# One small product folded in two, GpSimd's first work re-timed, and six products of ones at the start of a fused transformer kernel

## The chip, the cores and the metric

The kernel runs on one core of one Trainium2 chip. The time is device microseconds of one launch; less is better. Three runs of the kernel before gave 958.53, 959.26 and 959.52 us, median 959.26.

## What is computed

A whole decoder block stack in float32: four layers of attention with a feed-forward part, a cross attention, and a feed-forward part whose weights are put together from the 32 chosen of 64 primitives. Cut to what matters here:

```python
x = layernorm(x + attn_layers(x))        # 4 layers: local + linear attention, then gelu MLP
x = layernorm(x + cross_attention(x, ctx))
x = layernorm(x + composed_ffn(x))

def compose_weight(logits, A, B):        # "the choice", 64 logits, 32 taken
    vals, idx = top_k(logits, 32)
    w = softmax(vals)
    return einsum('k,kir,kro->io', w, A[idx], B[idx])
```

The choice depends on 64 logits alone, so the kernel makes it early, between the first attention's products, and uses its weights some 650 us later.

## The kernel before

Every engine runs a program written out by hand, and semaphores tie them together; nothing is scheduled by a tool. 2048 tokens are worked in four items of 512. Float32 products are made of three passes over a high part and a low part: ScalarE or GpSimd writes the high part, VectorE or GpSimd the low part (the "splits": `split_wo`, `split_lo`, lines L412 and L418).

`first_step` and `second_step` hold the first two items of layer 0, and beside them all the work that is done once. The order of instructions on an engine is the order in the code, so an engine that waits holds up everything behind it. The parts that matter here:

- **VectorE, `first_step`.** `top_choose` finds the rank of each logit and, last, writes `chosen` in two instructions (L782); their semaphore step is `top_step` 6. Then comes the reciprocal of the softmax sums of item 0 (L717). `top_weigh` follows: two instructions on the choice's sums and places in PSUM (L788, L789), `lw` (L792: product of two 64x2 tiles in SBUF), and `weighted` in two instructions (L795: SBUF to SBUF, by a scalar of each row), whose step is `top_w` 1. Behind them stand the low part of the linear attention (L635, one source in PSUM) and four copies of transposed probabilities out of PSUM (L713).
- **TensorE, `first_step`.** `top_k` (L1645, L1647) sums and gathers for the choice. Then the transposes of the first half's probabilities (`pe_pt`, L1559), then a wait for `index_ready` and for `top_w` 1, then `pe_pnorm` (L1566), the second half's transposes, a projection, `pe_pv` (L1576), two more projections, and `top_columns` (L1654), which spreads `weighted` over the partitions.
- **GpSimd.** After constants and the second item's `rstd` it waits for the choice, splits Wo (L412 twice, L418 twice), writes the low part of W1 (L418 four times) and adds the bias bo to item 0 (`pool_bias`, L470). The bias is needed by `dve_res1` (L733).
- **VectorE, `second_step`.** `dve_features` of item 1 begins with the query's maximum (L664) and the subtraction of it (L666, two sources in SBUF), whose step is `qsub_done` 2; this is "the query pass". Behind them are the score maxima out of PSUM (L707, L708), then L671 (SBUF to SBUF), L673, L676, L678 and L680. L680 releases TensorE's `pe_qnt` (L1526). L691 releases `pe_lin` (L1550), L631 the transposes of the second norm (L1453).
- **TensorE's beginning.** `pe_busy` (L1621) multiplies the bf16 identity by itself into PSUM; nobody reads the result. Seven such products wait for `const_step` 8, five more for the first `rstd`, and three follow the first transposes (L1638).

Of the kernel before, what the change touches and what calls it, by code (L numbers as in the profile page):

```python
# [19 lines left out]
P = 128  # L20
# [22 lines left out]
def build(nc, x_in, Wq, Wk, Wv, Wo, bo, ln1_g, ln1_b, W1, b1, W2, b2, ln2_g, ln2_b,  # L43
          ctx_in, Wkv, Wout, bout, fc1_A, fc1_B, fc2_A, fc2_B, fc1_logits, fc2_logits, out):
    with ExitStack() as ctx:
        def sb(name, shape, dt=F32):
            return ctx.enter_context(nc.sbuf_tensor(name, shape, dt))

        def sem(name):
            return ctx.enter_context(nc.semaphore(name))  # L50
# [21 lines left out]
        ones = sb("ones", [P, 1])  # L72
# [28 lines left out]
        weighted = top[:, 384:448].rearrange("p (f n) -> p f n", f=2)  # L101
        ones64, earlier = top[:, 640:768], top[:, 768:832]
# [35 lines left out]
        def f_ht(p, i, m):  # L138
# [3 lines left out]
            if i == 0:  # L142
# [5 lines left out]
        F = ctx.enter_context(nc.psum_tensor("F", [P, 2, 512], F32))  # L148
# [8 lines left out]
        const_step, const_ready, zero_ready = sem("const_step"), sem("const_ready"), sem("zero_ready")  # L157
# [14 lines left out]
        qmax_done, qsub_done, qexp_done, kexp_done = sem("qmax_done"), sem("qsub_done"), sem("qexp_done"), sem("kexp_done")  # L172
# [16 lines left out]
        logits_loaded, top_const, top_step, top_exp, top_w, top_idx, top_wcol, index_ready = (  # L189
            sem(n) for n in ("logits_loaded", "top_const", "top_step", "top_exp", "top_w", "top_idx",  # L190
                             "top_wcol", "index_ready"))
# [19 lines left out]
        def slot(p):  # L211
            return slice(TILES * p, TILES * p + TILES)

        def w1_part(k):


            c, s = k // 2, k % 2

            def dst(i):
                return w1[:, i, c, :].rearrange("q (m p) -> q p m", p=P)[:, 64 * s:64 * s + 64, :]  # L220
            return dst, A[:, k, :].rearrange("q (p m) -> q p m", m=FC)
# [15 lines left out]
        def cross_bank(u):  # L237
            return F[:, u - 2, :] if 2 <= u < 4 else A[:, u + 4 if u < 2 else u - 4, :]
# [49 lines left out]
        def _(sp):  # L288
# [49 lines left out]
            def indices(first):  # L338

                _, values = nc.values_load_multi_w_load_instructions(  # L340
                    index[0:1, bass.ds(first, 8)], engines=[mybir.EngineType.SP], min_val=0, max_val=PRIMS - 1,
                    skip_runtime_bounds_check_because="VectorE holds every index between 0 and PRIMS - 1 as it writes them")
                return values
# [70 lines left out]
        def split_lo(pool, pieces, hi_sem, ready, l):  # L414

            for k, (hi, low, src) in enumerate(pieces):
                pool.wait_ge(hi_sem, len(pieces) * l + k + 1)
                last = pool.tensor_tensor(low, src, hi.bitcast(F32), ALU.subtract)  # L418
            last.then_inc(ready, 1)
# [12 lines left out]
        def split_wo(pool, l, n=None):  # L432
            pool.wait_ge(raw_wo_loaded, 16 * (l + 1))
            if n is not None:
                pool.wait_ge(wo_psum, 2 * n + 2)
            split(pool, [(wo[:, 0, c, :], wo[:, 1, c, :], raw_a[:, c, 768:1024]) for c in range(DC)], wo_hi, wo_ready, l)
# [7 lines left out]
        def w1_pieces():  # L444
            hi, low = (w1[:, i].rearrange("p c n -> p (c n)") for i in range(2))
            return [(hi[:, a:a + TOK], low[:, a:a + TOK], raw_f[:, a:a + TOK]) for a in range(0, 2048, TOK)]
# [18 lines left out]
        def pool_bias(pool, i, n, p):  # L465

            vec = (vec_a, vec_f)[i]
            pool.wait_ge(ln_ready[i], TILES * (n + 1))
            pool.wait_ge(bias_loaded[i], 16 * (n // ITEMS + 1))
            pool.tensor_tensor(x[:, slot(p), :], x[:, slot(p), :], vec[:, 2:3, :].broadcast_to([P, TILES, D]),  # L470
                               ALU.add).then_inc(biased[i], 1)
# [7 lines left out]
        def _(pool):  # L479
# [36 lines left out]
            pool_rstd(pool, 0, 1)  # L516
            pool.wait_ge(zero_ready, 1)
            pool.wait_ge(top_const, 8)
            pool.wait_ge(top_w, 1)
            split_wo(pool, 0)  # L520
            split_lo(pool, w1_pieces(), w1_hi, w1_ready, 0)
            pool_bias(pool, 0, 0, 0)

            def step(l, p, attn=True, nxt=True, mlp=True, out=True):
# [54 lines left out]
            for k in range(4):  # L579
                dst, _ = w1_part(k)  # L580
                pool.wait_ge(comp_hi, k + 1)
                last = pool.tensor_tensor(dst(1), w1_raw[:, k, :].rearrange("q (p m) -> q p m", m=FC), dst(0).bitcast(F32),
                                          ALU.subtract)
# [1034 lines left out]
        def pe_busy(pe, bank, count):  # L1618

            for _ in range(count):  # L1620
                pe.matmul(bank.rearrange("p (k n) -> p k n", k=4), ident_bf[:, :],  # L1621
                          ident_bf[:, :].rearrange("p (o n) -> p o n", o=1).broadcast_to([P, 4, P]), start=True, stop=True)

        @block.tensor
        def _(pe):
            pe.wait_ge(const_step, 8)
            pe_busy(pe, F[:, 1, :], 7)
            pe.wait_ge(const_ready, 1)
# [20 lines left out]
            def top_columns():  # L1649
                pe.wait_ge(top_w, 1)  # L1650
                pe.wait_ge(tok_out, 5)
                for j in range(2):
                    for f in range(2):
                        last = pe.matmul(F[:, 0, 32 * j + 16 * f:32 * j + 16 * f + 16], ones64[:, :],  # L1654
                                         weighted[:, f, :].rearrange("i (k j) -> i j k", j=2)[:, j, :], start=True, stop=True)
                last.then_inc(top_wcol_psum, 1)

            def wvt_turn(k):
# [15 lines left out]
            def first_step():  # L1674
# [39 lines left out]
                pe_tok(pe, 1, 2)  # L1714
                pe_tok(pe, 1, 3)
                top_columns()
                pe_s(pe, 1, 0)
                pe.wait_ge(tok_out, 8)
# [200 lines left out]
            for u in range(2 * ITEMS):  # L1919
# [6 lines left out]
                for i in range(2):  # L1926
                    last = pe.matmul(cross_bank(u)[:, D:2 * D], pick[:, u:u + 1].broadcast_to([P, P]), mean_row[i],
                                     start=i == 0, stop=i == 1)
# [68 lines left out]
```

## Time and profile before

| | |
|---|---|
| median of 3 runs | 959.26 us (958.53 to 959.52) |
| the profiled execution's own time | 958.49 us |
| its span, first to last instruction | 956.3 us |
| TensorE busy | 944.4 us, 99% |
| VectorE, ScalarE, GpSimd busy | 673.6, 611.8, 480.2 us |
| chain that ended last | 94% TensorE, 3% VectorE, 1% ScalarE, 1% issue |

How to read it: the 2.2 us between the span and the own time lie around the instructions. The chain that ended last is followed back from the last instruction, so a microsecond taken off a part of the chain counts in full until a second chain of nearly the same length shows up. All that the change touches lies in the first 62 us; after that the program is the same.

### The profile page before, as it was taken

The numbers are of one execution on the slowest core, as the hardware profiler recorded it, in microseconds if no ns is written. First come the engines' busy times: TensorE is split into PE (matmuls) and PEld (weight loads), VectorE is DVE, ScalarE is ACT, GpSimd is POOL, SyncE is SP. The second block draws the span as 40 slices with busy tenths as digits, with TensorE's granted clock in tenths as the row PEclk, the third lists the DMA queues.
The fourth block names the chain that finished last, engine by engine and source line by source line (L and its number), as shares of the span: only waits on it lengthen the run. The fifth ranks groups of instructions, "written<-read, shape, count | busy, mean of one in ns | idle before, by whom it ended". The sixth has DMA issues, their size and how long they took to land.

```text
span 956.3 us, 21341 instructions
## 1 busy us (share of the span) xinstructions
PE 944.4 (99%) x8394; PEld 815.6 (85%) x8394; DVE 673.6 (70%) x1529; ACT 611.8 (64%) x1389; POOL 480.2 (50%) x381
## 2 busy tenths in 40 slices
PE   7999999999999999999999999999999999999998
PEld 4688888888888889888888888888997889998997
DVE  7796868677777868696777678776662776666445
ACT  4777777686776867777768677686856345444220
POOL 3437375456826472775466367816247224006453
PEclk9999999999999999999999999999999999999999
DMA  6231000001110000021000003000028696820001
GB/s 211 72 108 45 2 17 2 8 11 58 33 45 19 2 1 19 1 89 45 10 9 1 18 2 84 4 2 7 2 57 204 137 205 143 181 46 1 23 23 45
DMA packets 71582, 47.56 MB, mean 50 GB/s; under 512 B 44511, under 2 KB 68159, under 8 KB 71487
## 3 DMA queue, kind: packets, MB, share of 16 engines
q1 hardware_dynamic: 71487, 46.27, 18.9%
q8 instruction: 63, 1.03, 0.4%
q14 instruction: 32, 0.26, 0.1%
HBM read 44.16 MB, written 2.10 MB: 48 GB/s over the span
## 4 chain that ended last, share of the span: by engine, by line
PE 94%; DVE 3%; ACT 1%; issue 1%; DMA 0%; POOL 0%; SPq 0%; POOLq 0%; DVEq 0%; ACTq 0%
PE F L1460 21%; PE F L1614 19%; PE A L1460 16%; PE A L1802 5%; PE A L1795 5%; PE A L1559 4%; PE A L1955 4%; PE A L1517 3%; PE F L1474 2%; PE A L1576 2%; PE A L1474 2%; PE F L1453 2%; PE A L1550 1%; PE A L1453 1%; PE A L1533 1%; PE A L1526 1%
## 5 line engine op out<-in xcount | busy, mean ns | idle before, releaser
L1460 PE MATMUL F<-xt,w 128*128 128x512 f32 x864 | 217.8, 400 | 0.2 <-ACT scratch L1211 0.2
L475 POOL TENSOR_TENSOR ht<-scratch,ht 128x512 fp32r<-128x512 f32 x128 | 176.2, 1397 | 29.4 <-ACT ht L1214 27.9
L1460 PEld LDWEIGHTS F<-xt,w 128*128 128x128 f32 x864 | 157.6, 188 | 38.2 <-issue 3.0
L1614 PE MATMUL F<-w,ht 128*128 128x256 f32 x1536 | 188.8, 282 | 0.0
L1614 PEld LDWEIGHTS F<-w,ht 128*128 128x128 f32 x1536 | 182.8, 188 | 5.3 <-issue 4.6
L463 POOL TENSOR_TENSOR rstd<-var,minus_half 128x4 f32<-128x4 f32 x32 | 37.6, 1173 | 176.4 <-DVE var L611 175.8
L1211 ACT ACTIVATE scratch<-F,b_now 128x512 f32<-128x512 f32 x128 | 87.6, 684 | 36.6 <-POOL ht L475 19.0
L1460 PE MATMUL A<-wa,xt 128*128 128x512 f32 x372 | 89.8, 397 | 0.0
L470 POOL TENSOR_TENSOR x<-x,vec_f 128x1024 f32<-128x1024 f32 x16 | 38.0, 2376 | 93.7 <-DVE scratch L631 93.7
L1214 ACT ACTIVATE ht<-scratch 128x512 fp32r<-128x512 f32 x128 | 80.9, 632 | 4.1
L1460 PEld LDWEIGHTS A<-wa,xt 128*128 128x128 f32 x372 | 69.0, 188 | 15.9 <-issue 0.2
L631 DVE SCALAR_TENSOR_TENSOR scratch<-scratch,rstd,vec_a 128x256 f32<-128x256 f32 x64 | 70.3, 1158 | 0.2
L1182 ACT ACTIVATE prob<-A,smax 128x128 f32<-128x128 f32 (+1 forms) x128 | 51.9, 432 | 21.5 <-DVE smax L708 21.5
L1149 ACT ACTIVATE scratch<-A 128x256 f32<-128x256 f32 x62 | 23.7, 382 | 63.8 <-PE A L1460 63.5
L635 DVE TENSOR_TENSOR xt<-A,xt 128x512 fp32r<-128x512 f32 x52 | 33.5, 685 | 39.2 <-ACT xt L1134 34.4
L733 DVE TENSOR_TENSOR x<-A,x 128x512 f32<-128x512 f32 x30 | 20.7, 692 | 54.4 <-PE A L1460 54.4
L1444 ACT ACTIVATE scratch<-F 128x512 f32<-128x512 f32 x32 | 19.2, 600 | 54.1 <-PE F L1460 48.4
L1182 ACT ACTIVATE scratch<-A,smax 128x128 f32<-128x128 f32 (+1 forms) x128 | 51.9, 434 | 0.4
L740 DVE TENSOR_TENSOR x<-F,x 128x256 f32<-128x256 f32 x64 | 26.4, 420 | 32.3 <-PE F L1614 32.3
L563 POOL TENSOR_TENSOR trstd<-tvar,minus_half 128x4 f32<-128x4 f32 (+1 forms) x15 | 13.3, 887 | 68.2 <-DVE tvar L835 68.2
L603 DVE BATCH_NORM_STATS2 stats<-x 128x6 f32<-128x256 f32 x128 | 44.8, 413 | 2.2 <-DMA x<-in_x_dram 1.6
L1460 PEld LDWEIGHTS A<-wo,at 128*128 128x128 f32 x360 | 43.3, 188 | 1.3
(264 smaller groups left out, 2041.9 us busy)
## 6 DMA issues: line engine op xcount, KB each, us to landing
raw_f<-in_L_attn_W_dram SPq DMA_DIRECT2D x8, 1024.0 KB, 5.5
scratch<-in_L_ffn_fc_B_dram SPq DMA_DIRECT2D x32, 256.0 KB, 4.2
scratch<-in_L_ffn_fc_A_dram SPq DMA_DIRECT2D x32, 256.0 KB, 4.0
raw_f<-in_L_ffn_fc_A_dram SPq DMA_DIRECT2D x32, 64.0 KB, 3.4
scratch<-in_x_dram SPq DMA_DIRECT2D x1, 2048.0 KB, 10.1
raw_f<-in_L_ffn_fc_B_dram SPq DMA_DIRECT2D x32, 64.0 KB, 3.2
x<-in_x_dram SPq DMA_DIRECT2D x3, 512.0 KB, 3.7
out_dram<-x SPq DMA_DIRECT2D x3, 512.0 KB, 2.9
```

Source lines behind the costliest of these rows:

```text
L475: pool.tensor_tensor(ht[:, 1, m, :], hf[:, m % 2, :], ht[:, 0, m, :].bitcast(F32), ALU.subtract).then_inc(h_lo, 1)
L603: last = dve.bn_stats(stats[i][:, t, :], x[:, TILES * p + t, :])
L631: dve.scalar_tensor_tensor(out=xh[i][:, t, :], in0=xh[i][:, t, :], scalar=rstd[i][:, t:t + 1], in1=vec[:, 1, :], op0=ALU.mult, op1=ALU.add ...
L1182: last = act.activation(prob[b][:, h, a:z], A[:, 2 + h, a:z], ACT.Exp, bias=smax[:, b, w, h:h + 1], scale=-1.0, accum_out=psums[:, 2 * b + ...
L1211: act.activation(hf[:, m % 2, :], F[:, m % 2, :], ACT.Gelu, bias=b1_now[:, m:m + 1]).then_inc(gelu_done, 1)
L1214: act.activation(ht[:, 0, m, :], hf[:, m % 2, :], ACT.Copy).then_inc(h_hi, 1)
L1460: last = pe.matmul(out, lhs(a, c), rhs(b, c), start=clear and k == 0, stop=k == len(total) - 1, skip_group_check=not clear)
L1474: last = pe.matmul(out, lhs(a, c), rhs(b, c), start=k == 0, stop=k == len(total) - 1)
L1559: last = pe.transpose(A[:, PT_BANKS[b][r], P * h:P * h + P], prob[b][:, h, P * r:P * r + P], ident[:, :])
L1614: last = pe.matmul(F[:, t % 2, 0:D], ht[:, a, c, P * t:P * t + P], w2[:, b, c, :], start=k == 0, stop=k == len(passes) - 1)
L1795: last = pe.matmul(A[:, 2 * c + s, :], small[r][a][:, P * c:P * c + P], big[r][b][:, 512 * s:512 * s + 512], start=first and k == 0, stop= ...
L1802: last = pe.matmul(A[:, m // 2, D * (m % 2):D * (m % 2) + D], big[r][a][:, P * m:P * m + P], small[r][b], start=first and k == 0 and m % 2 ...
```

## The change

Four edits. GpSimd's first split waits for `top_step` 6 (the ranks' `chosen`) where it waited for `top_w` 1 (the finished weights). GpSimd's first bias sum waits for `qsub_done` 2 as well. TensorE begins with six products of a column of ones, spread with stride 0 to 128x128, as soon as the ones are written (`const_step` 1). And `top_columns` makes one product of 32 columns for each half `j` where it made two of 16 columns (two `matmul` calls instead of four; a float32 product leaves two records, so four records instead of eight).

```diff
             pool_rstd(pool, 0, 1)
             pool.wait_ge(zero_ready, 1)
             pool.wait_ge(top_const, 8)
-            pool.wait_ge(top_w, 1)
+            pool.wait_ge(top_step, 6)
             split_wo(pool, 0)
             split_lo(pool, w1_pieces(), w1_hi, w1_ready, 0)
+            pool.wait_ge(qsub_done, 2)
             pool_bias(pool, 0, 0, 0)
...
         @block.tensor
         def _(pe):
+            pe.wait_ge(const_step, 1)
+            for _ in range(6):
+                pe.matmul(F[:, 1, 0:P], ones[:, :].broadcast_to([P, P]), ones[:, :].broadcast_to([P, P]), start=True, stop=True)
             pe.wait_ge(const_step, 8)
             pe_busy(pe, F[:, 1, :], 7)
...
                 for j in range(2):
-                    for f in range(2):
-                        last = pe.matmul(F[:, 0, 32 * j + 16 * f:32 * j + 16 * f + 16], ones64[:, :],
-                                         weighted[:, f, :].rearrange("i (k j) -> i j k", j=2)[:, j, :], start=True, stop=True)
+                    last = pe.matmul(F[:, 0, 32 * j:32 * j + 32].rearrange("p (f k) -> p f k", f=2), ones64[:, :],
+                                     weighted[:, :, :].rearrange("i f (k j) -> i j f k", j=2)[:, j], start=True, stop=True)
                 last.then_inc(top_wcol_psum, 1)
```

On GpSimd, from the constants of the mask to the second norm's bias, with the semaphores that each instruction waits for:

```order
 L514 AFFINE_SELECT mask_seed<-mask_seed 128x128 x2
 L463 TENSOR_TENSOR rstd<-var,minus_half 128x4 [waits ln1_var]
-L412 TENSOR_TENSOR wo<-raw_a,ones 128x256 [waits top_w,raw_wo_loaded,top_const,zero_ready]
+L412 TENSOR_TENSOR wo<-raw_a,ones 128x256 [waits top_step,raw_wo_loaded,top_const,zero_ready]
 L412 TENSOR_TENSOR wo<-raw_a,ones 128x256
 L418 TENSOR_TENSOR wo<-raw_a,wo 128x256 [waits wo_hi] x2
 L418 TENSOR_TENSOR w<-raw_f,w 128x512 [waits w1_hi] x4
-L470 TENSOR_TENSOR x<-x,vec_a 128x1024 [waits bo_loaded,ln1_ready]
+L470 TENSOR_TENSOR x<-x,vec_a 128x1024 [waits bo_loaded,ln1_ready,qsub_done]
```

No instruction of GpSimd moved against another; two of them wait for something else.

On TensorE around `top_columns`, in the kernel before (the last projection ahead of it is L1460, the scores of item 1 behind it L1510 and L1517):

```order
L1460 MATMUL A<-wa,xt 128x512 [waits aloc_done]
L1460 MATMUL A<-wa,xt 128x512 x5
L1654 MATMUL F<-scratch 128x16 [waits tok_out,top_w]
L1654 MATMUL F<-scratch 128x16 x3
L1510 MATMUL A<-mask_bf,ident_bf 64x2x128 x8
L1517 MATMUL A<-kT,qT 128x128 x4
```

and in the changed kernel:

```order
L1461 MATMUL A<-wa,xt 128x512 [waits aloc_done]
L1461 MATMUL A<-wa,xt 128x512 x5
L1657 MATMUL F<-scratch 128x32 [waits tok_out,top_w]
L1657 MATMUL F<-scratch 128x32
L1511 MATMUL A<-mask_bf,ident_bf 64x2x128 x8
L1518 MATMUL A<-kT,qT 128x128 x4
```

Two of the four products went, and the two that stay have twice the columns.

## Rows read from the trace of the kernel before

**Rows 1.** The page: the span.
```profile
span 956.3 us, 21341 instructions
```

**Rows 2.** Chain that ended last, 33 to 62 us: start us, us, what.
```profile
33.09 0.04 issue
33.13 0.87 PE A L1550 x48
...
37.47 0.44 PE A L1566 x4
...
45.05 0.99 PE F L1654 x8
```

**Rows 3.** Timeline of TensorE: start us, us, instructions.
```profile
37.30 0.60 PE L1566 MATMUL A<-ident,scratch 128*128 128x128 f32 x4
...
52.67 0.60 PE L1526 MATMUL A<-ident,scratch 128*128 128x128 f32 x4
...
61.69 1.05 PE L1453 MATMUL F<-ident,scratch 128*128 128x128 f32 x8
```

**Rows 4.** Timeline of VectorE, the choice.
```profile
34.48 0.37 DVE L782 TENSOR_SCALAR scratch<-places,rank 64x32 f32<-64x32 f32 x2
...
36.25 0.14 DVE L792 TENSOR_TENSOR lw<-lexp,lsum 64x2 f32<-64x2 f32 x1
36.43 0.38 DVE L795 TENSOR_SCALAR scratch<-scratch,lw 64x32 f32<-64x32 f32 x2
```

**Rows 5.** Timeline of GpSimd, its first splits and bias sum.
```profile
37.04 1.18 POOL L412 TENSOR_TENSOR wo<-raw_a,ones 128x256 fp32r<-128x256 f32 x2 [18.65 <-DVE scratch L795]
38.18 1.43 POOL L418 TENSOR_TENSOR wo<-raw_a,wo 128x256 fp32r<-128x256 f32 x2
39.55 5.04 POOL L418 TENSOR_TENSOR w<-raw_f,w 128x512 fp32r<-128x512 f32 x4
44.55 2.81 POOL L470 TENSOR_TENSOR x<-x,vec_a 128x1024 f32<-128x1024 f32 x1
```

**Rows 6.** Timeline of VectorE, item 1's query pass and what follows.
```profile
46.50 1.40 DVE L666 TENSOR_TENSOR scratch<-scratch,qmax 128x512 f32<-128x512 f32 x1
...
49.69 0.41 DVE L671 TENSOR_SCALAR scratch<-scratch 128x512 f32<-128x512 f32 x1
...
51.74 0.69 DVE L680 TENSOR_TENSOR scratch<-scratch,qsum 128x512 f32<-128x512 f32 x1
...
59.91 1.67 DVE L631 SCALAR_TENSOR_TENSOR scratch<-scratch,rstd,vec_f 128x256 f32<-128x256 f32 x4
```

**Rows 7.** VectorE's L611 by itself: ns min/median/max, first and last start.
```profile
L611 DVE TENSOR_SCALAR var<-mv x32: 169/170/622, 5.5 to 706.3; 128x4 f32<-128x4 f32 x32
```

**Rows 8.** Timelines of VectorE and GpSimd at three meetings later in the run.
```profile
88.50 0.62 DVE L611 TENSOR_SCALAR var<-mv 128x4 f32<-128x4 f32 x1
87.78 1.31 POOL L418 TENSOR_TENSOR w<-raw_f,w 128x512 fp32r<-128x512 f32 x1
...
228.95 1.54 DVE L671 TENSOR_SCALAR scratch<-scratch 128x512 f32<-128x512 f32 x1
228.93 1.28 POOL L418 TENSOR_TENSOR w<-raw_f,w 128x512 fp32r<-128x512 f32 x1
...
71.36 0.48 DVE L631 SCALAR_TENSOR_TENSOR scratch<-scratch,rstd,vec_a 128x256 f32<-128x256 f32 x1
71.35 1.64 POOL L475 TENSOR_TENSOR ht<-scratch,ht 128x512 fp32r<-128x512 f32 x1
```

**Rows 9.** TensorE's beginning: its timeline, then a stretch's sums (granted clock after POOL's).
```profile
3.44 3.17 PE L1621 MATMUL F<-ident_bf 128*128 128x512 bf16 x7 [3.44 <-POOL ident_bf L490]
7.14 1.84 PE L1621 MATMUL F<-ident_bf 128*128 128x512 bf16 x5 [0.54 <-POOL rstd L463]
9.44 1.63 PE L1638 MATMUL A<-ident,scratch 128*128 128x128 f32 x8 [0.46 <-DVE scratch L631]
...
3.40:6.70 3.30, 3.17 (x7) 0.88 (x7) 2.01 (x10) 0.00 (x0) 2.78 (x9) 1.00 0.76 215
```

## The prediction, made before the changed kernel ran

> **What bounds the kernel now.** I began with the page: a span of 956.3 us [rows 1], and TensorE at 99% busy. A kernel like that gains only what leaves TensorE's own queue, and loses whatever makes TensorE wait. So the second view was the chain that ended last, over the stretch that the change touches [rows 2]. The reader is to see that from 33.13 us, when the wait for VectorE's context ended ("issue" 0.04), to 61.85 us it is TensorE alone, product after product. Third came the timelines of TensorE, VectorE and GpSimd side by side at the places of the edits [rows 3 to 6], to see how much room each releaser has. Fourth, meetings of VectorE and GpSimd elsewhere in the run [rows 7, 8], since the edits put GpSimd's work beside other instructions of VectorE.
>
> **A. `top_columns`.** It leaves eight records in 0.99 us of the chain [rows 2], 0.124 each. Four go: 0.50 us. The four that stay have 32 columns instead of 16; L1566's transposes have 128 columns and take 0.44/4 = 0.11 each [rows 2], so the wider columns cost between nothing and nothing visible. TensorE is on the chain here, so 0.5 us comes off, for as long as nobody else is late. ScalarE's copy of the weights behind it comes earlier too, and waits for nothing else.
>
> **B. GpSimd's splits come earlier.** L782 ends at 34.48 + 0.37 = 34.85 [rows 4]. Today L795 ends at 36.81 and the first split starts at 37.04 [rows 4, 5], 0.23 later. With the same 0.23 it will start at 35.08, 1.96 earlier. Nobody waits for the splits: the product with Wo starts at about 48 us, so the earliness itself earns nothing. What counts is who is met. By the durations of [rows 5], L412 runs 35.08 to 36.26, the two L418 on Wo 36.22 to 36.95 and 36.91 to 37.65, the first on W1 37.59 to 38.88, and all is done by 42.6.
>
> VectorE has L792 at 36.25 and L795 at 36.43 [rows 4], between `top_k` and the wait at which TensorE wants `top_w`. What does it cost to meet GpSimd? [Rows 8] show it. L611, a small SBUF to SBUF operation of 0.17 us by itself [rows 7], takes 0.62 at 88.50 and ends at 89.12, just after GpSimd's L418 (87.78 + 1.31 = 89.09). L671, 0.41 by itself [rows 6], takes 1.54 at 228.95 and ends at 230.49, 0.28 after GpSimd's 228.93 + 1.28 = 230.21. So VectorE's instruction is held until GpSimd's ends, and then needs its own duration less about 0.13. Who starts first decides: L671 started 0.02 behind GpSimd's and lost; L631 at 71.36, 0.01 behind GpSimd's 71.35, took its plain 0.48, and GpSimd's took 1.64.
>
> The Trainium skill speaks against this edit: its GPSIMD Engine Reference, § 1 Specifications, says that GpSimd's SBUF interfaces are shared with VectorE, with contention for VectorE instructions that have two SBUF inputs or run in a two-port mode. The trace agrees for L611 and L671, which have a single tensor in SBUF. If only two-input instructions were held, L792 alone would pay, and the sum below would shrink to the second rival's 0.5 us.
>
> Step by step then. L792 wants to start at 36.25, 0.03 behind L418's 36.22: nearer to the lost meeting (0.02) than to the won one (0.01), so it is held to 36.95 and ends at 36.95 + 0.14 - 0.13 = 36.96. The first L795 needs `lw`, so it starts at 36.99, 0.08 behind the second L418 (36.91): held to 37.65, done at 37.65 + 0.23 - 0.13 = 37.75. (0.23 is the pair's 0.38 less the 0.15 by which its starts lie apart.) The second L795 starts about 0.08 before that, at 37.67, 0.08 behind the first W1 split (37.59): held to 38.88, done at 38.98. TensorE's L1566, which starts at 37.30 today [rows 3], starts 0.05 after that (the 0.04 of "issue", rounded up [rows 2]): 39.03. **That is a new wait of 1.73 us on the chain.** Bounds: nothing, if VectorE wins each meeting (TensorE is only 0.45 behind `top_w` now: 36.81 + 0.05 against 37.30); 2.4 us if a GpSimd instruction is itself stretched by 0.3 as at 71.35 on the way, twice. Behind L795 on VectorE stand L635 and the L713 copies, which have PSUM sources. The first L713 would end near 40.1; the second half's last transposes, which wait for it and start 1.3 us after L1566, come at 40.3. So nothing is added there; everything behind moves by 1.73 as a block.
>
> **C. The bias sum behind the query pass.** Now it runs from 44.55 to 47.36 [rows 5], and L666 takes 1.40 [rows 6], 0.7 of it held (46.50 until 47.36). L666 will take 0.69. But the bias sum then starts 0.2 after it, at 47.19 + 0.2 = 47.4 (on the old clock), and runs about 2.4 us (2.81 less the 0.4 for which VectorE's L635 had just cut in) to 49.8. The score maxima read PSUM and pass. L671 comes 0.7 earlier, at 49.0, meets it, and ends at 49.8 + 0.41 - 0.13 = 50.05 instead of 50.10. So of 0.7 us VectorE keeps 0.05 to 0.1: the stall goes from L666 to L671. ScalarE does get its exponentials 0.7 earlier, which nobody waits for.
>
> That limits A. L680 ends at 52.43 now and releases L1526 at 52.67 [rows 3, 6], a slack of 0.24 with 0.05 taken by the release. Half a microsecond earlier, TensorE would want L680 by 52.12, and gets it at 52.35 + 0.05 = 52.40: A keeps 0.27 of its 0.5. VectorE works without a break from there, and L631 ends at 61.58 now against L1453 at 61.69: 0.06 of slack. Ended 0.08 earlier it lets TensorE be 0.14 earlier. **A and C together: -0.15 us** (between 0 and -0.5, if the bias sum does not meet L671).
>
> **D. Six products of ones.** TensorE stands idle until 3.44 [rows 9]; they fill 0.97 to about 3.6 (12 records of a float32 product at twice the 0.11 of A, since the engine is slow here). The seven fillers take 0.43 each, (3.17 - 0.61)/6, and of the five after them the last are quicker; the granted clock of that stretch reads 1.00, so what was really granted must be told from durations: the slower level (1.2 GHz) until after 8 us, the faster one (2.4 GHz) at 9.44. The transposes there wait for VectorE. So in this execution D earns nothing; it costs nothing while the fillers still end before 7.1, and they do with 0.4 to spare.
>
> The Trainium skill's TensorE: Matmul & The Clock Gate, Part 1, says that how many products are slow at a kernel's start varies from run to run. Here it would mean that some runs before paid in their first real products and the changed kernel does not; one trace can't show that.
>
> **Sum.** +1.73 - 0.15 + 0 = +1.6 us. Against the profiled execution's own 958.49 that is 960.1. The median of the three runs is 0.77 above it, and I take that difference to stay: 959.26 + 1.6 = **960.8 us**. A change within 0.2%, 1.9 us, is about what measurement of this kernel can't tell from none; so the forecast is "no difference", on its slow side.
>
> **Rivals.**
> - *The main case*, TensorE waits 1.7 us for `top_w`: +1.6, spread 0.5. For it: both rows of lost meetings, and lags of 0.03, 0.08, 0.08. Against it: the first lag is two hundredths from a won one, and a start that moves by 0.03 turns it. Chance 45%.
> - *One or two meetings won*: L792 wins its meeting, one L795 is held by the first Wo split, the other by the second. `top_w` at 37.65 + 0.1 = 37.75, TensorE at 37.80 instead of 37.30: +0.5 - 0.15, about 959.6. Chance 22%.
> - *No wait at all*, because such small tiles slip in: only A and C are left, -0.15 to -0.5, 958.9. Chance 18%. If the runs before also lose time to a slow start that D removes, 958.4, since their own spread is 1.0 us.
> - *The other side, slower by over 0.2%*: a clock that falls. With the ones ahead, the fillers may end by 5.5 us, and TensorE then stands idle to 7.14 and again to 9.44, or it idles 1.7 us at 37.3; if it is then back at the slower level, the first projections (24 or so of 0.235 us that would take 0.43) cost 2.5 us or more. It decides from about ten slow products on. For it: the idle stretches grow. Against it: no gap of 0.5 to 0.75 us had this effect in the first 12 us. Chance 8%, 962 to 963.
> - *Something that I did not see*: 7%, half on each side.
>
> **How the numbers follow.** Of the main case 30% lies over +1.9 us (a start or two more of 0.15 to 0.3), which with the clock gives slower 0.14 + 0.08 + 0.03 = 0.25. Faster by over 0.2% needs no wait, all of A and a slow start in the median: 0.08. The rest, 0.67, is no difference. The range leaves out the falling clock and the luckiest end: 958.6 to 962.0.
>
> **What would show it.** Right: GpSimd's first L412 at 35.1; L792 or L795 at several times 0.14 and 0.23; L1566 with an idle stretch released by VectorE's `weighted`; L666 at 0.69 and L671 near 1.0; the bias sum near 2.4 us; four records of `top_columns` in 0.5 us; L1526 waiting for L680. Wrong: L795 at its plain duration with GpSimd's split running, no idle in front of L1566, or fillers and first transposes at other durations than now.

## The result

The changed kernel takes 960.74 us, median of 14 runs (959.95 to 962.46), against 958.93 of 14 runs of the kernel before (957.81 to 959.77). The ratio is 1.0023, 95% interval 1.0016 to 1.0030: slower, by about the 0.2% that was called the bound of what can be told. Fourteen runs of each tell it from none all the same. The forecast of 960.8 us lies 0.06 from the median. The profiled execution took 962.04 us, near the top of its runs, with a span of 959.9; why it lies above the median comes out below. Two executions of the experiments' lots, at 1155.24 and 1869.04 us, stand far outside and are left out of every ratio and count below.

The page of the changed kernel begins:

```profile
span 959.9 us, 21357 instructions
PE 947.1 (99%) x8402; PEld 818.1 (85%) x8402; DVE 675.1 (70%) x1529; ACT 611.5 (64%) x1389; POOL 479.2 (50%) x381
```

TensorE is busy 2.7 us more than before with eight records more, and the span grew by 3.6 us [rows 1]. Where it went is read from the chain that ended last, 33 to 62 us, that answers to [rows 2] (start us, us, what):

```profile
34.80 0.87 PE A L1551 x48
...
37.67 1.46 PE A L1560 x12
39.13 1.54 issue
40.67 0.63 PE A L1567 x4
...
48.45 0.56 PE F L1657 x4
...
55.72 0.12 issue
55.84 0.63 PE A L1527 x4
```

L1567 is L1566 of before. In front of it stands 1.54 us of "issue", where before nothing stood. `top_columns` takes 0.56 instead of 0.99, and a small wait of 0.12 in front of L1527 (L1526 of before) is new. "issue" says that the trace names no releaser: the wait is for `index_ready` and `top_w`, which a sequencer's instruction takes. Who was late is seen on VectorE. Its timeline in the changed kernel, and below it GpSimd's:

```profile
37.92 0.71 DVE L793 TENSOR_TENSOR lw<-lexp,lsum 64x2 f32<-64x2 f32 x1
38.67 1.90 DVE L796 TENSOR_SCALAR scratch<-scratch,lw 64x32 f32<-64x32 f32 x2
40.49 0.54 DVE L636 TENSOR_TENSOR at<-A,at 128x384 fp32r<-128x384 f32 x1
...
36.75 1.18 POOL L412 TENSOR_TENSOR wo<-raw_a,ones 128x256 fp32r<-128x256 f32 x2 [17.45 <-DVE scratch L783]
37.89 1.42 POOL L418 TENSOR_TENSOR wo<-raw_a,wo 128x256 fp32r<-128x256 f32 x2
39.27 5.00 POOL L418 TENSOR_TENSOR w<-raw_f,w 128x512 fp32r<-128x512 f32 x4
50.67 2.40 POOL L470 TENSOR_TENSOR x<-x,vec_a 128x1024 f32<-128x1024 f32 x1 [6.41 <-DVE scratch L667]
```

L793 (before: L792) takes 0.71 instead of 0.14, and the two L796 (before: L795) 1.90 together instead of 0.38 [rows 4]. The second L796 and the W1 split that it meets, each by itself:

```profile
39.27 1.30 DVE L796 TENSOR_SCALAR scratch<-scratch,lw 64x32 f32<-64x32 f32 x1
...
39.27 1.27 POOL L418 TENSOR_TENSOR w<-raw_f,w 128x512 fp32r<-128x512 f32 x1
```

They start in the same hundredth of a microsecond, and VectorE's ends 0.03 after GpSimd's. GpSimd's first split starts 0.23 after L783 has ended, as forecast, and its splits run through all three of VectorE's instructions. L636, with a source in PSUM, takes its usual 0.54 in the middle of a W1 split. The bias sum takes 2.40 and stands behind the query pass:

```profile
49.90 0.69 DVE L667 TENSOR_TENSOR scratch<-scratch,qmax 128x512 f32<-128x512 f32 x1
...
52.37 0.99 DVE L672 TENSOR_SCALAR scratch<-scratch 128x512 f32<-128x512 f32 x1
```

The query pass is at 0.69 instead of 1.40 [rows 6], and L672 (before: L671) at 0.99 instead of 0.41, just as the forecast had it.

So much was in the prediction. The beginning was not. Timeline of TensorE in the changed kernel, then sums of 9 to 20 us, with the granted clock after GpSimd's:

```profile
0.96 2.93 PE L1629 MATMUL F<-ones 128*128 128x128 f32 x12 [0.96 <-POOL minus_half L481]
3.68 2.23 PE L1622 MATMUL F<-ident_bf 128*128 128x512 bf16 x7
7.14 1.24 PE L1622 MATMUL F<-ident_bf 128*128 128x512 bf16 x5 [1.23 <-POOL rstd L463]
10.29 1.79 PE L1642 MATMUL A<-ident,scratch 128*128 128x128 f32 x8 [1.90 <-DVE scratch L632]
11.87 1.49 PE L1622 MATMUL F<-ident_bf 128*128 128x512 bf16 x3
13.37 2.40 PE L1475 MATMUL A<-xt,wa 128*128 128x512 f32 x6
...
9.00:20.00 11.00, 9.70 (x36) 6.67 (x37) 10.16 (x40) 3.97 (x8) 1.19 (x1) 0.84 0.95 293
```

The fillers at 3.68 and 7.14 are quicker than in [rows 9], so the clock rose earlier. But the three fillers at 11.87 take 1.49 us and the first six products 2.40; with the kernel before they take 0.81 and 1.64. The granted clock over 9 to 20 us is 0.84, so a part of that stretch ran at the slower level (1.2 GHz). TensorE had idled for 1.23 and 1.90 us ahead of it. The first transposes also start at 10.29, 0.85 later than in the profiled execution of before, because a layer norm's vector landed 0.4 us later and VectorE worked through it more slowly. Kernels with and without the ones have both early and late starts of this kind (9.0 to 10.3 us in fourteen profiled executions), so that part is taken to be of the execution, not of the change.

Against the trace of before, instruction by instruction, TensorE is late by 0.84 us at the first transposes, 0.82 more when the slow stretch is over, and 1.70 more at L1567. It gets back 0.20 by L1527, and loses 0.39 near 420 us, which comes out below. Together that is the growth of the span but for a few hundredths.

### The profile page after: what moved, and what is told of

The parts are those of the page before. It is cut to its first block, busy times and chain, and to the rows that moved or that the text cites. A ratio compares the mean times of both kernels' runs of the same rounds, so it can differ in the third digit from the quotient of the medians.

```text
span 959.9 us, 21357 instructions
## 1 busy us (share of the span) xinstructions
PE 947.1 (99%) x8402; PEld 818.1 (85%) x8402; DVE 675.1 (70%) x1529; ACT 611.5 (64%) x1389; POOL 479.2 (50%) x381
## 4 chain that ended last, share of the span: by engine, by line
PE 94%; DVE 3%; issue 1%; ACT 1%; DMA 1%; POOL 0%; SPq 0%; POOLq 0%; DVEq 0%; ACTq 0%
PE F L1461 21%; PE F L1615 19%; PE A L1461 16%; PE A L1805 5%; PE A L1798 5%; PE A L1560 4%; PE A L1958 4%; PE A L1518 3%; PE F L1475 2%; PE A L1475 2%; PE A L1577 2%; PE F L1454 2%; PE A L1551 1%; PE A L1454 1%; PE A L1534 1%; PE A L1527 1%
## 5 line engine op out<-in xcount | busy, mean ns | idle before, releaser
L636 DVE TENSOR_TENSOR xt<-A,xt 128x512 fp32r<-128x512 f32 x52 | 33.5, 686 | 39.5 <-ACT xt L1135 34.8
```

## The experiments

Twelve kernels, in three lots; within a lot they share a chip and the runs of the kernel before (medians 958.64, 958.66 and 958.58 us). All ratios are against those runs, with 95% intervals about 0.001 to each side, so a difference of 0.9 us is what one of them can tell. Each kernel has one trace, of one execution; "late" and "early" are against the trace of the kernel before.

### The splits alone

```diff
-            pool.wait_ge(top_w, 1)
+            pool.wait_ge(top_step, 6)
             split_wo(pool, 0)
```

> The kernel before with the split's earlier start alone. Theory (VectorE's small tiles are held while GpSimd's splits run): L792 and both L795 at 0.7 to 1.3 us, an idle of 1.5 us in front of L1566, +1.7 us. Rival (the slower clock at the start made the difference, the wait is only in the trace): +0.2 or less.

Measured: 960.25 us, ratio 1.0018 (1.0009 to 1.0027), slower. In its trace TensorE's first transposes start 0.59 later than in that of before (10.03 against 9.44) and L1566 starts 2.29 later (39.59 against 37.30): 1.70 came at the wait. This part by itself makes most of the loss: +1.6 us in the median, where the changed kernel has +1.8.

### The splits put back

```diff
-            pool.wait_ge(top_step, 6)
+            pool.wait_ge(top_w, 1)
             split_wo(pool, 0)
```

> The changed kernel with the splits behind the finished weights again, so two-product columns, later bias sum and ones. Theory: no hold at L792 and L795, L1567 starts 0.5 after the records before it, -0.1 to -0.4 us against before. Rival (the ones cost, by a clock that falls): +0.5 to +0.9 us.

Measured: 958.82 us, ratio 1.0003 (0.9994 to 1.0012), where the changed kernel has 1.0023. No wait stands in front of `pe_pnorm`. The later bias sum, the columns and the ones together can't be told from nothing; the rival's +0.5 to +0.9 lies within the interval at its upper half, so a cost of the ones is not excluded here.

### Only Wo's high parts behind the ranks

```diff
             pool.wait_ge(top_step, 6)
-            split_wo(pool, 0)
+            wo_pieces = [(wo[:, 0, c, :], wo[:, 1, c, :], raw_a[:, c, 768:1024]) for c in range(DC)]
+            pool.wait_ge(raw_wo_loaded, 16)
+            split_hi(pool, wo_pieces, wo_hi)
+            pool.wait_ge(top_w, 1)
+            split_lo(pool, wo_pieces, wo_hi, wo_ready, 0)
             split_lo(pool, w1_pieces(), w1_hi, w1_ready, 0)
```

> The changed kernel, but of GpSimd's splits only the two high parts of Wo (L412) run behind the ranks; all low parts wait for the finished weights. Theory: L412 has just ended when L792 starts, so no hold and no wait at pnorm: 1.7 us less than the changed kernel, about -0.1 to +0.3 against before. Rival (an earlier GpSimd costs by whatever it does): still +1.7.

Measured: 958.87 us, ratio 1.0004 (0.9995 to 1.0013). VectorE's timeline of this kernel, then GpSimd's (its lines lie 4 further down):

```profile
36.12 0.14 DVE L797 TENSOR_TENSOR lw<-lexp,lsum 64x2 f32<-64x2 f32 x1
36.30 0.38 DVE L800 TENSOR_SCALAR scratch<-scratch,lw 64x32 f32<-64x32 f32 x2
...
34.97 1.19 POOL L412 TENSOR_TENSOR wo<-raw_a,ones 128x256 fp32r<-128x256 f32 x2 [16.70 <-DVE scratch L787]
36.76 1.43 POOL L418 TENSOR_TENSOR wo<-raw_a,wo 128x256 fp32r<-128x256 f32 x2 [0.61 <-DVE scratch L800]
```

GpSimd starts 2 us earlier than before and works on the high parts from 34.97 to 36.16, and VectorE's three instructions take their plain 0.14 and 0.38. Their only overlap is the last 0.04 us of L412, too short to show. It isn't the earliness that costs, but GpSimd's instructions running beside these three.

### TensorE no longer waits for the weights at pnorm

```diff
-                pe.wait_ge(top_w, 1)
+                pe.wait_ge(top_step, 7)
                 pe_pnorm(pe, 0)
```

> The changed kernel, where TensorE's wait in front of L1567 asks for the sum of the choice (top_step 7) and no longer for the finished weights. If the wait at that place were the whole cost: 1.7 us less than the changed kernel. Theory: VectorE's queue itself is late, its first L714 copy ends about 2.2 later than before, and the last transposes of the second half wait for it, so all but 0.2 us of the stall comes back two instructions later: +1.5 against before.

Measured: 960.99 us (9 runs), ratio 1.0024 (1.0014 to 1.0034), as the changed kernel. Timeline of TensorE:

```profile
37.12 0.60 PE L1567 MATMUL A<-ident,scratch 128*128 128x128 f32 x4
37.55 1.04 PE L1560 MATMUL A<-ident,prob 128*128 128x128 f32 x8
39.84 0.66 PE L1560 MATMUL A<-ident,prob 128*128 128x128 f32 x4 [1.25 <-DVE scratch L714]
```

The wait in front of L1567 is gone, and 1.25 us of idle stands two groups later, ended by VectorE's L714 copy. Against the trace of before TensorE is 0.17 early at L1567 and 1.23 late behind that wait: 1.40 of the 1.70 came back. It is VectorE's queue that is late; the semaphore only shows where TensorE notices it first. The run also names the wait: the "issue" in front of L1567 was for `top_w`, since it goes when that wait goes.

### The changed kernel without the ones

```diff
-            pe.wait_ge(const_step, 1)
-            for _ in range(6):
-                pe.matmul(F[:, 1, 0:P], ones[:, :].broadcast_to([P, P]), ones[:, :].broadcast_to([P, P]), start=True, stop=True)
```

> The changed kernel without the six products of ones: splits behind the ranks, later bias sum, two-product columns. Theory (the ones cost about half a microsecond to one by a falling clock, the hold 1.7): +1.3 to +1.6 us against before, the wait in front of L1566 unchanged at 1.5. Rival (the ones cost nothing in the median): +1.8 as the changed kernel.

Measured: 960.14 us, ratio 1.0014 (1.0005 to 1.0023). The waits of TensorE from 20 to 80 us (who for whom, us in total, times, longest) hold the one at pnorm and nothing else that is new:

```profile
PE A L1567 <- issue: 1.5, 1, 1.5
```

In this trace TensorE is 0.08 late at the first transposes, 1.79 at L1567 (1.82 behind it), 1.39 behind `top_columns`, 1.60 at L1527 and 1.65 at the second norm's transposes (L1454, L1453 of before), where the prediction drew its sum. Those are its steps one by one: +1.71, -0.43, +0.21, and in all +1.57 over the start, where the sum had +1.58.

### The ones alone

```diff
         def _(pe):
+            pe.wait_ge(const_step, 1)
+            for _ in range(6):
+                pe.matmul(F[:, 1, 0:P], ones[:, :].broadcast_to([P, P]), ones[:, :].broadcast_to([P, P]), start=True, stop=True)
```

> The kernel before with the six products of ones alone. Forecast of the prediction: 0 in most executions. Rival, from the trace of the changed kernel: the products at 11.9 to 15.1 us at the slower clock in a part of the executions, +0.8 us in those, a wider spread upwards and +0.2 to +0.8 in the median.

Measured: 959.81 us, ratio 1.0011 (1.0002 to 1.0020), +1.2 us in the median. The prediction's zero falls here. TensorE's beginning in this kernel:

```profile
10.03 1.62 PE L1641 MATMUL A<-ident,scratch 128*128 128x128 f32 x8 [1.65 <-DVE scratch L631]
11.49 1.24 PE L1621 MATMUL F<-ident_bf 128*128 128x512 bf16 x3
13.05 2.36 PE L1474 MATMUL A<-xt,wa 128*128 128x512 f32 x5 [0.32 <-DVE xt L635]
```

Again the first products run slowly, with a granted clock of 0.84 over 9 to 20 us. TensorE is 0.59 late when the transposes start and 1.53 when the slow stretch is over: 0.94 for the clock. A further 0.83 comes at 420 us (below).

But this trace is of the slowest of the kernel's eleven executions, and the record shows that it doesn't speak for the others. Every execution of the changed kernel and of the experiments' lots has a mean granted clock on record. The four traces in which a part of 9 to 20 us is at the slower level have 0.997 or 0.998, the ten others 0.999 or 1.000, so the executions with such a fall can be counted without a trace:

| kernels | executions | at 0.998 or less |
|---|---|---|
| the kernel before, three lots | 96 | 20 |
| six other kernels without the ones | 65 | 8 |
| the five kernels with the ones and the usual fillers | 56 | 7 |
| the ones and more fillers | 11 | 0 |
| the ones and fewer fillers | 11 | 11 |

A fall costs: the 20 executions of before have a median of 959.31 us, the 76 others 958.48. But the ones with the usual fillers don't make it more frequent, 7 of 56 against 20 of 96. Of the eleven executions here only the profiled one has it; the ten others have a median of 959.76 us, and the 26 executions of before in this lot without a fall 958.46. So the ones cost about a microsecond in executions in which the clock stayed up, and the falling clock isn't what their median pays for.

### The ones with more fillers, and with fewer

```diff
-            pe_busy(pe, F[:, 1, :], 7)
+            pe_busy(pe, F[:, 1, :], 14)
...
-            pe_busy(pe, F[:, 1, :], 5)
+            pe_busy(pe, F[:, 1, :], 9)
```

> The kernel before with the six products of ones, and with fourteen and nine fillers of identity products in place of seven and five, so that TensorE has hardly an idle stretch before its first transposes. If the ones cost through TensorE's idleness after an early rise of the clock: no product at the slower level after the first transposes, and 0 to +0.3 us against before instead of +1.1. If the ones cost through their own reading of SBUF or their place in the queue: still +1 us. If the fillers come late to the transposes, these start late by up to 0.4.

Measured: 959.30 us, ratio 1.0006 (0.9997 to 1.0015). In the trace TensorE works almost without a break to the transposes, the granted clock of 9 to 20 us is 1.00, and the products are at their usual duration:

```profile
3.68 5.94 PE L1621 MATMUL F<-ident_bf 128*128 128x512 bf16 x23
9.46 1.26 PE L1641 MATMUL A<-ident,scratch 128*128 128x128 f32 x8
10.55 0.81 PE L1621 MATMUL F<-ident_bf 128*128 128x512 bf16 x3
12.11 1.64 PE L1474 MATMUL A<-xt,wa 128*128 128x512 f32 x6 [0.75 <-DVE xt L635]
```

None of the eleven executions shows a fall. Their median is all the same 0.9 us over that of the 24 executions of before in this lot without a fall (958.38), and the profiled execution, at 958.09, is the fastest of the eleven: its trace doesn't show what the others pay. So the expectation's second case, a cost of the ones that has nothing to do with the clock, isn't excluded.

The other way round, without the five fillers behind the first rstd:

```diff
             pe.wait_ge(ln_rstd[0], 1)
-            pe_busy(pe, F[:, 1, :], 5)
```

> The kernel before with the six products of ones, and without the five identity products behind the first rstd, so that TensorE idles from about 6 us to its first transposes. Theory (an idle stretch after an early rise brings the clock down): products at the slower level among the first projections in nearly every execution, +1 to +2 us against before. Rival (the ones cost by being there): +1.1 as with them alone, and no slower level in the trace.

Measured: 959.65 us, ratio 1.0008 (0.9999 to 1.0017). The trace shows an idle stretch of 2.74 us, then slow transposes and fillers:

```profile
9.00 1.94 PE L1640 MATMUL A<-ident,scratch 128*128 128x128 f32 x8 [2.74 <-DVE scratch L631]
10.73 1.49 PE L1621 MATMUL F<-ident_bf 128*128 128x512 bf16 x3
12.22 1.69 PE L1474 MATMUL A<-xt,wa 128*128 128x512 f32 x6
```

The clock came down, as expected, in this and in all ten other executions (mean granted clocks 0.996 to 0.998). In the trace TensorE lost 0.27 by it, over work that has other waits beside it; but that execution, at 958.31, is the fastest of the eleven, and the median is +1.1 us (the ratio's interval -0.1 to +1.6), at the low end of the expected +1 to +2 or under it. The rival's "no slower level in the trace" is refuted, its +1.1 is not. No kernel without the ones has the five fillers taken out, so it isn't shown that the early start is needed for the fall. The intervals of the three kernels with ones overlap, and their order isn't shown.

### Columns and bias, together and each alone

The kernel before, with the columns' edit, the bias sum's, or both:

```diff
             split_lo(pool, w1_pieces(), w1_hi, w1_ready, 0)
+            pool.wait_ge(qsub_done, 2)
             pool_bias(pool, 0, 0, 0)
...
                 for j in range(2):
-                    for f in range(2):
-                        last = pe.matmul(F[:, 0, 32 * j + 16 * f:32 * j + 16 * f + 16], ones64[:, :],
...
+                    last = pe.matmul(F[:, 0, 32 * j:32 * j + 32].rearrange("p (f k) -> p f k", f=2), ones64[:, :],
...
```

Both:

> The kernel before with the two-product columns and the later bias sum alone. Prediction's term: -0.15 us, with L671 held to about 1.0 us by the bias sum. Rival (the bias sum is free of the query pass and meets nothing): -0.5 us. Should be the fastest of the parts, and not to be told from before.

Measured: 958.70 us, ratio 0.9997 (0.9988 to 1.0006). In the trace TensorE starts 0.12 late, is 0.31 early behind the columns, 0.11 at L1526 and 0.06 at L1453 [rows 3]: over its start -0.43, -0.23 and -0.18. The columns:

> The kernel before with the two-product columns alone. Prediction's term: 0.5 us at the columns' place, seen at the scores right behind them; about half of it lost again at L1526, which then waits for VectorE's L680; at the end 0 to -0.3 us, not to be told from before. Rival (the room behind is wide): -0.5 us kept.

Measured: 958.34 us, ratio 0.9999 (0.9989 to 1.0008). Timeline of TensorE:

```profile
44.97 0.63 PE L1653 MATMUL F<-scratch 64*128 64x32 f32 x4
45.52 0.41 PE L1510 MATMUL A<-mask_bf,ident_bf 64*64 64x256 bf16 x8
...
52.57 0.63 PE L1526 MATMUL A<-ident,scratch 128*128 128x128 f32 x4 [0.19 <-DVE scratch L680]
```

Behind the columns TensorE is 0.45 early; at L1526 it waits 0.19 for L680 and starts at 52.57 instead of 52.67 [rows 3]. Of 0.45 us, 0.10 is left. The bias sum:

> The kernel before with the later bias sum alone. Prediction's term: L666 at 0.69 instead of 1.40, L671 at 1.0 instead of 0.41, L680 ending 0.1 earlier, TensorE where it was: 0.0 us. Rival (the query pass was on the path): -0.5 us.

Measured: 958.73 us, ratio 1.0000 (0.9991 to 1.0010). TensorE doesn't move. VectorE meets the bias sum at L672 alone:

```profile
46.93 0.69 DVE L667 TENSOR_TENSOR scratch<-scratch,qmax 128x512 f32<-128x512 f32 x1
...
49.62 0.76 DVE L672 TENSOR_SCALAR scratch<-scratch 128x512 f32<-128x512 f32 x1
...
47.70 2.39 POOL L470 TENSOR_TENSOR x<-x,vec_a 128x1024 f32<-128x1024 f32 x1 [2.68 <-DVE scratch L667]
```

L672 takes 0.76 and not 1.0 because it begins 2.00 behind the end of L667, where in the changed kernel it is 1.78 (52.37 less 50.59). The bias sum has 0.47 left then (to 50.09), there 0.70 (to 53.07). 0.47 and 0.70 plus the plain 0.41, less 0.12, are the two measured durations, 0.76 and 0.99: the hold is the rest of GpSimd's instruction.

This kernel has no ones, and yet its profiled execution shows a slow stretch over the first transposes and the three fillers (granted clock 0.84 over 9 to 20 us):

```profile
9.54 1.95 PE L1639 MATMUL A<-ident,scratch 128*128 128x128 f32 x8 [1.14 <-DVE scratch L632]
11.29 1.48 PE L1622 MATMUL F<-ident_bf 128*128 128x512 bf16 x3
```

TensorE lost 0.32 by it. So the clock can come down without the ones too, as the count above has it for one execution of before in five.

### What costs nothing, together

The changed kernel with only Wo's high parts early, as above, and no ones. On that kernel with the low parts put back:

```diff
-            pe.wait_ge(const_step, 1)
-            for _ in range(6):
-                pe.matmul(F[:, 1, 0:P], ones[:, :].broadcast_to([P, P]), ones[:, :].broadcast_to([P, P]), start=True, stop=True)
             pe.wait_ge(const_step, 8)
```

> The changed kernel without the ones, and with only the two high parts of Wo behind the ranks (all low parts behind the finished weights): what is left is what costs nothing. Theory: no hold, no wait, no slow stretch: -0.1 to -0.4 us against before, which can't be told from none; 1.3 us or more under the changed kernel.

Measured: 958.12 us, ratio 0.9996 (0.9986 to 1.0005), the lowest median of all, 2.6 us under the changed kernel, and not to be told from the kernel before.

## Why the prediction held, and where it didn't

- **The main case came as forecast, step by step.** L793 started 0.03 behind GpSimd's split and lost that meeting; each L796 lost its own. The wait was worked out as 1.73 us; three traces show 1.70, 1.70 and 1.71. That VectorE's small tiles are held while GpSimd's instruction runs is shown by the low parts put back (hardly an overlap, no hold); that the hold is the whole cost, by the wait that moved when TensorE asked for less. What the trace doesn't bear out is the reading of the lag: L631 won with a lag of 0.01, and the second L796 lost with none (both start at 39.27). Which of two that start within a hundredth wins can't be read from these starts.
- **What was said to follow from it, did.** L636 and the L714 copies, which read PSUM, weren't held; the stall moved the rest as a block.
- **Columns and bias: -0.15 forecast, -0.18 and -0.17 at L1453 in two traces** (both edits alone, and the changed kernel without the ones). The step "A keeps 0.27 of its 0.5" was right in kind, 0.23 and 0.22 measured: TensorE runs into L680 at L1526, and the stall of the query pass goes on to L671. The prediction's sum for L671 has a slip: 49.8 + 0.41 - 0.13 is 50.08 and not 50.05, which leaves VectorE 0.02 instead of 0.05 to 0.1 and the term at -0.08 to -0.1. So some of the closeness is luck. No timing could tell the term from nothing.
- **"D earns nothing, it costs nothing" is the step that failed.** The ones alone cost 1.2 us in the median (0.2 to 1.9). The sign for it had been named: fillers at other durations than before, and they came at 2.23 and 1.24 us instead of 3.17 and 1.84 [rows 9].
- **The falling clock is real, but it isn't what the ones cost.** The rival put it at 2.5 us or more and 8%. It came down in two of the five profiled kernels that have the ones and the usual fillers, both times those whose transposes started late (10.03 and 10.29 us; the others 9.01 to 9.31), and TensorE lost 0.82 and 0.94 by it. In the changed kernel three of fourteen executions have it, and they are its three slowest (961.79 to 962.46). But by the counts above it comes about as often without the ones, so it explains the profiled execution and not the median. Nor did the ones take away what some executions of before pay at their start, which the prediction had as a possible gain. Behind idle stretches it is a matter of the single execution: with 0.55 and 1.11 us of idle ahead of the transposes it stayed up in the changed kernel without the ones, with 0.70 and 1.14 it fell in the bias sum's.
- **What the ones cost with the clock up is open.** The one other difference that traces show: in four of the seven traces of kernels with ones TensorE pauses in the middle of transposes near 420 us, with nobody late; in none of the seven without. In the changed kernel:

```profile
421.80 0.38 PE L1560 MATMUL A<-ident,scratch 128*128 128x128 f32 x2
422.41 1.25 PE L1560 MATMUL A<-ident,scratch 128*128 128x128 f32 x10 [0.23 <-issue]
```

Twelve transposes that took 1.47 us in one go with the kernel before are cut in two, though the program is the same there, and TensorE is 0.40 later behind them (0.83 with the ones alone, 0.68 with the splits put back, 0.36 where TensorE waits for the sum). The six products add 24 records to the program, 12 products and 12 weight loads. A transfer of instructions by the DMA falls within 418 to 422 us in every trace, with the pause or without. That the fetching of TensorE's program is what pauses it is a guess, which no run here tests; and the kernels with more and with fewer fillers, whose programs are longer too, show no pause in their traces. Those two traces and that of the low parts put back, the three without a pause, are each 0.6 to 1.4 us under their kernel's median. That would fit a pause in most executions, but isn't shown.
- **The number.** The sum gave +1.6 without any cost of the ones, and the changed kernel without the ones has +1.5 in its median (1.0014) and +1.57 in its trace. The ones should add 1.2 to that by the run with them alone; in the changed kernel the medians leave 0.3 for them and the ratios 0.9, with intervals that overlap, so their share there isn't settled. Against the median that was known then, 959.26, the forecast of 960.8 came out 0.06 from what was measured, but fourteen runs of before have their median at 958.93. The difference is 1.8 us by the medians and 2.2 by the ratio (1.5 to 2.9), not 1.6. A base that was 0.33 too high made up for a cost that was left out: the closeness is partly luck. And "no difference", which was given 0.67, is not what the runs say: the interval excludes none, and it has 0.2% inside it.

## What to carry to other kernels

Before an operation of GpSimd is moved earlier, look at what VectorE does in those microseconds: small SBUF to SBUF operations that something waits for cost what is left of the GpSimd instruction beside them, whatever their own size. A saving on the busiest engine is worth only as much as the next releaser has room; read it from the timeline before counting it (here 0.45 became 0.10). And work that only warms TensorE up is not free because TensorE was idle: the six products cost 1.2 us in the median, and the traces account for a part of it only. Last, a trace is one execution. Where every execution's mean clock is at hand, count how many share what the trace shows before the median is explained by it.

## What the runs showed of the hardware

- A product of 64x2 on VectorE took 0.71 us instead of 0.14, and a scaling of 64x32 took 0.68 and 1.30 instead of 0.23, beside GpSimd's 0.73 and 1.27. VectorE's copies and reductions out of PSUM, and those with one source there, took their usual time beside the same instructions (L636 0.54, L714 0.64 each, L709 0.68). VectorE's second L796 started at the same hundredth as GpSimd's W1 split (39.27), and lost.
- With work from 0.96 us TensorE's clock rose earlier: the seven fillers took 2.03 to 2.57 us in the five traces with the ones and the usual fillers and in that with fewer, and 3.00 to 3.17 in the seven without the ones. In the changed kernel it came down at about 11.6 us, after idle stretches of 1.23 and 1.90 us; in the kernel with the bias sum alone at about 9.6, after 0.70 and 1.14; and it stayed up with 1.51 and 0.53 (the splits put back). The Trainium skill's TensorE: Matmul & The Clock Gate, § HAM oscillation, tells of a clock that falls each time TensorE has waited for data between short bursts of products. The trace agrees in that the fall came behind idle stretches, 1.23 and 1.90 us; the counts add that it takes one execution of a kernel and spares another.
- A pause of 0.36 to 0.83 us near 420 us inside a run of transposes, with no releaser, in four of seven traces of kernels that have six more products in the first 4 us, and in none of seven others.
